# Graph kernel, adjacency build on one core: target one-hots compared in pairs of columns for the first two quarters

## What is computed

```
edge_index = jnp.stack([src, dst])
h = jnp.maximum(_layernorm(x, axis=-1), 0.0)
x = x + _L0_gnn_ref(h, edge_index, ...)        # aggr = segment_sum(x[src], dst)
...
x = x + _L3_gnn_ref(h, edge_index, ...)
```

## Time and profile before

| | us |
|---|---|
| median of 3 runs | 1218.46 (1216.65 to 1220.22) |
| the profiled execution's own time | 1211.5 |
| its span | 1209.6 |
| build, quarter 0 (halves 0 to 13) | 22.8 to 88.5 |
| build, quarter 1 (halves 14 to 27) | 88.5 to 150.0 |
| build, quarters 2 and 3 | 150.0 to 281.5 |

### The profile page before, as it was taken

How to read it: one execution, slowest core, us unless ns; L and a number is a source line. 1 busy time by engine, 2 the same in 40 slices (tenths; PEclk the granted TensorE clock), 3 DMA queues, 4 the chain that set the end, 5 groups by cost and what they waited for, 6 DMA issues and landing times.

```text
span 1209.6 us, 19346 instructions
## 1 busy us (share of the span) xinstructions
PE 1128.0 (93%) x6308; PEld 658.0 (54%) x6308; DVE 678.4 (56%) x2170; ACT 454.7 (38%) x1347; POOL 11.0 (1%) x36
## 2 busy tenths in 40 slices
PE   3778899999999999999899898998899999999997
PEld 3556666665564554545545445545555556544644
DVE  7999999995563235446255355355654325632211
ACT  4559988886562112211301311203521214811100
POOL 1000000000000000000000000000000000000000
PEclk9999899999999999999899999999899999999999
DMA  2100000001101013433134123299942313500001
GB/s 76 24 1 2 2 2 10 1 2 34 22 10 25 19 39 80 91 76 77 39 69 89 33 64 84 61 252 190 211 96 69 85 37 102 132 26 26 16 22 31
DMA packets 208277, 70.33 MB, mean 58 GB/s; under 512 B 180949, under 2 KB 207284, under 8 KB 208174
## 3 DMA queue, kind: packets, MB, share of 16 engines
q1 hardware_dynamic: 124702, 42.31, 16.1%
q10 hardware_dynamic: 83152, 25.52, 9.5%
q0 software_dynamic: 320, 1.22, 0.6%
HBM read 20.71 MB, written 28.26 MB: 40 GB/s over the span
## 4 chain that ended last, share of the span: by engine, by line
PE 81%; DVE 10%; DMA 3%; ACT 2%; issue 2%; ACTq 1%; DVEq 0%; SPq 0%
PE PS L1190 51%; PE PS L894 8%; DVE HPb L758 4%; PE PS L2647 4%; PE PS L883 2%; PE PS L1567 2%; PE PS L859 2%; DMA di_d<-SM 2%; PE PS L2097 2%; PE PS L2103 2%; DVE HPb L709 2%; PE PS L2135 1%; PE PS L1685 1%; PE PS L1235 1%; PE PS L888 1%
## 5 line engine op out<-in xcount | busy, mean ns | idle before, releaser
L1190 PE MATMUL PS<-ADJ,HPb 125*128 125x500 bf16 (+2 forms) x2250 | 447.3, 354 | 0.0
L1190 PEld LDWEIGHTS PS<-ADJ,HPb 125*128 125x128 f16 x2250 | 219.4, 98 | 223.4 <-issue 32.1
L930 ACT CAST ADJ<-PS 126x72 f32 (+7 forms) x784 | 193.4, 316 | 53.8 <-PE PS L894 18.8
L1190 PE MATMUL PS<-ADJ,Zf 125*128 125x500 bf16 (+2 forms) x1050 | 202.1, 352 | 0.0
L894 PE MATMUL PS<-HPb 128*128 128x150 bf16 (+3 forms) x784 | 193.5, 350 | 3.0 <-ACT ADJ L930 2.4
L1190 PEld LDWEIGHTS PS<-ADJ,Zf 125*128 125x128 f16 x1050 | 102.4, 98 | 93.8 <-issue 1.3
L758 DVE TENSOR_SCALAR HPb<-XRf,Zf 128x176 bf16<-128x176 f16 (+2 forms) x588 | 135.8, 289 | 1.7 <-PE PS L894 0.7
L883 PEld LDWEIGHTS PS<-HPb 128*128 128x128 bf16 x642 | 86.3, 142 | 62.5 <-issue 37.5
L1871 DVE CUSTOM_DVE_ANT_0 HPb<-ADJ,HPb 125x625 bf16<-125x625 bf16 x125 | 101.3, 811 | 3.7
L883 PE MATMUL PS<-HPb 128*128 128x25 bf16 x642 | 91.5, 215 | 12.6 <-DVE HPb L758 11.8
L1977 DVE BATCH_NORM_STATS2 WB<-PS 128x6 f32<-128x500 f32 (+2 forms) x28 | 17.7, 630 | 144.8 <-PE PS L2103 144.8
(11 more groups left out here) (340 smaller groups left out, 1077.1 us busy)
## 6 DMA issues: line engine op xcount, KB each, us to landing
adj_d<-ADJ ACTq DMA_DIRECT2D x25, 700.0 KB
HPb<-y_d SPq DMA_DIRECT2D x19, 187.5 KB, 2.5
HPb<-di_d SPq DMA_DIRECT2D x10, 250.0 KB, 3.4
adj_d<-ADJ ACTq DMA_DIRECT2D x25, 81.2 KB
ADJ<-in_x SPq DMA_DIRECT2D x1, 1562.5 KB
q_d<-HPb SPq DMA_DIRECT2D x25, 62.5 KB
HPb<-di_d SPq DMA_DIRECT2D x5, 305.2 KB
HPb<-s_d ACTq DMA_DIRECT2D x5, 250.0 KB, 3.7
```

What stands on the lines that cost most here:

```text
L930: e.copy(to, WPS[group % BANKS][0:PD, t0 * RESTS[q]:t1 * RESTS[q]] .rearrange("p (t d) -> p t d", t=t1 - t0)).then_inc(s_mv, 1)
L1190: mm = e.matmul(accs[q], H[0:PN, t, q, 0:P], cols, start=(t == 0 and (two or q == 0)), stop=(t == NT - 1 and (two or q == 1)), skip_group_ ...
```

## The change

In quarters 0 and 1 (`PAIRED = 2`) one TENSOR_TENSOR compares two columns at once: it reads `IOK[q]`, now with every number stored twice, and the two columns' keys from a new f16 table `KTH[q]`, broadcast along the numbers, and writes the two one-hots interleaved element by element into one slot of the ring. The ring of 7 slots so holds 14 columns. PE reads a column's one-hot as every second element of the slot. Quarters 2 and 3 are as before.

```diff
+    PAIRED = 2
+    IOS = [w * (2 if k < PAIRED else 1) for k, w in enumerate(KWS)]
...
+        def key_pair(q, m):
+            return OHK[m // 2 % RING][:, 0:IOS[q]].rearrange("p (w c) -> p w c", c=2)
+
+        def key_hot(q, m):
+            return key_pair(q, m)[:, :, m % 2] if q < PAIRED else OHK[m % RING][:, 0:KWS[q]]
...
-                    line(e.tensor_copy(IOK[k], iota_i[:, c0:c0 + KWS[k]]))
+                    numbers = iota_i[:, c0:c0 + KWS[k]]
+                    if k < PAIRED:
+                        numbers = numbers.rearrange("p (w o) -> p w o", o=1).broadcast_to([P, KWS[k], 2])
+                    line(e.tensor_copy(IOK[k], numbers))
...
-            tables = ((KT, til_f, (2, 0)), (PT, src_f, (3, 1)), (KGT, key_f, (6, 7)))
+            tables = ((KT, til_f, (6, 7)), (PT, src_f, (3, 1)), (KGT, key_f, (2, 0)))
...
+                keys_told(0)
+                table_out(1)
...
+                table_out(2)
                 e.wait_ge(s_frow, 1)
                 e.copy(IOC, IOP.rearrange("p (n o) -> p n o", o=1).broadcast_to([P, P, HC])).then_inc(s_rowc, 1)
+                table_out(0)
+                keys_told(1)
...
+                    if n == 2 * QS:
+                        e.wait_ge(s_rowc, KR + 13)
                     for m in range(HC):
-                        k = (h * HC + m) % RING
-                        if m % 2 == 0:
-                            e.wait_ge(s_ohx, n0 + m + 2)
+                        free = n0 + m + 2 - (RING if q < PAIRED else 0)
+                        if m % 2 == 0 and free > 0:
+                            e.wait_ge(s_ohx, free)
...
+                        elif m % 2 == 0:
+                            e.tensor_tensor(key_pair(q, n0 + m), IOK[q],
+                                            KTH[q][:, n0 + m - q * KTW:n0 + m + 2 - q * KTW].rearrange("p (o c) -> p o c", o=1)
+                                            .broadcast_to([P, KWS[q], 2]), ALU.is_equal).then_inc(s_oh, 2)
...
-                                              OHK[m % RING][:, 0:NT], start=False, stop=True, skip_group_check=True)
+                                              key_hot(q, m)[:, 0:NT], start=False, stop=True, skip_group_check=True)
...
-                                     OHK[m % RING][:, NTP:KWS[q]], start=(c == 0), stop=(c == GC - 1),
+                                     key_hot(q, m)[:, NTP:KWS[q]], start=(c == 0), stop=(c == GC - 1),
```

More of the change, by code:

```diff
@@ L148, in build @@
         OHW = -(-KWP // 64) * 64
+        assert GC == 2 and RING == HG and all(w <= OHW for w in IOS)
         IOW = sum(KWS[:3]) + P
+        KTW = GC * QG
         SRW = max(RW, HC * P // 2)
@@ L153, in build @@
         HPb = sb("HPb", [P, max(NT * 2 * FW + 2048, RING * OHW + 2 * HC * P + NT * GW, 8 * RW, 60 * P)], BF16)[:, :]
-        XRf = sb("XRf", [P, max(NT * P, RW + SRW + sum(KWS[:2]) // 2 + 8 + P // 2 + GW * NT // 2 + FTW)], F32)[:, :]
+        XRf = sb("XRf", [P, max(NT * P, RW + SRW + sum(IOS[:2]) // 2 + GW * NT // 2 + 2 + FTW)], F32)[:, :]
         Zf = sb("Zf", [P, max(NT * P, 3 * NCH + (NCH + HC) // 2, 25 * P)], F32)[:, :]
@@ L227, in build @@
         c0 = RW + SRW
[L228 to L232, removed]
+        IOK = [XRf[:, c0:c0 + IOS[0] // 2].bitcast(F16),
+               XRf[:, c0 + IOS[0] // 2:c0 + (IOS[0] + IOS[1]) // 2].bitcast(F16)]
+        IOK = [v.rearrange("p (w c) -> p w c", c=2) for v in IOK]
+        c0 += -(-(IOS[0] + IOS[1]) // 8) * 4
+        IOP = HPb[:, 8 * RW + 8 + KTW:8 * RW + 8 + KTW + P].bitcast(F16)
         IOL = XRf[:, c0:c0 + GW * NT // 2].bitcast(F16)
@@ L237, in build @@
         FT = XRf[:, c0:c0 + FTW].bitcast(I32)
+        KTH = [HPb[:, 8 * RW + 8:8 * RW + 8 + KTW].bitcast(F16),
+               WB[:, 4 * P + 6 * NT + 2:4 * P + 6 * NT + 2 + KTW // 2].bitcast(F16)]
         dst_f, src_f, til_f, key_f = (HPf[0:QG, k * RW:(k + 1) * RW] for k in range(4))
@@ L601, in program, with keys_told, table_out @@
             if act:
-                for n, (tab, _, banks) in enumerate(tables):
+                def keys_told(q):
+                    for h in range(GC):
+                        e.wait_ge(s_rowt, h + 1)
+                        e.copy(KTH[q].rearrange("p (g h) -> p g h", h=GC)[:, :, h],
+                               PS[:, tables[0][2][h], q * QG:(q + 1) * QG]).then_inc(s_rowc, 1)
+                def table_out(n):
+                    tab, _, banks = tables[n]
                     for h in range(GC):
@@ L606, in program @@
                          .then_inc(s_rowc, 1)
[L607 to L610, removed]
+                keys_told(0)
+                table_out(1)
+                for h in range(GC):
+                    e.copy(PTH[:, 0:NCH].rearrange("p (g h) -> p g h", h=GC)[:, :, h], PS[:, tables[1][2][h], 0:G])\
+                     .then_inc(s_rowc, 1)
+                table_out(2)
                 e.wait_ge(s_frow, 1)
                 e.copy(IOC, IOP.rearrange("p (n o) -> p n o", o=1).broadcast_to([P, P, HC])).then_inc(s_rowc, 1)
+                table_out(0)
+                keys_told(1)
             e.wait_ge(s_flag, 1)
@@ L887, in half @@
                             else:
-                                e.matmul(CPS[h][:, g * NT:(g + 1) * NT], lhs, OHK[m % RING][:, 0:NT], start=(c == 0),
+                                e.matmul(CPS[h][:, g * NT:(g + 1) * NT], lhs, key_hot(q, m)[:, 0:NT], start=(c == 0),
                                          stop=(c == GC - 1), skip_group_check=True)
@@ L969, in general_build @@
             if role == "pool":
-                e.wait_ge(s_rowc, KR + 9)
+                e.wait_ge(s_rowc, KR + 13)
                 line = Line(e, s_gpool)
```

5 lines of the change are left out of this document (3 added, 2 removed).

## The result

| | before | after |
|---|---|---|
| median of the timed runs, same chip, us | 1218.38 (1216.65 to 1220.22) | 1212.07 (1210.74 to 1212.79) |
| ratio to before, 95% interval | 1 | 0.9949 (0.9935 to 0.9964) |
| profiled execution: own time, span | 1211.5, 1209.6 | 1212.8, 1211.2 |
| quarter 0, us | 65.7 | 58.8 |
| quarter 1, us | 61.5 | 60.8 |

The kernel is faster by 6.3 us. The forecast was 14.7 us (1204), with a range down to a gain of 6.5. The sign is right and the size is less than half. The last four lines use one cut everywhere: a quarter runs from the start of the source one-hots of its first half (line 709 before, 736 after) to the next quarter's, and the build ends where DVE's first 125x1500 instruction starts. (The 131.5 of the earlier trace rows for the last two quarters stops at 281.5; by this cut it is 132.1.)

A forecast was written before the change was run, and what follows sets the result against it. DVE alone was taken to set quarter 0, and DVE with 3.2 us of waits quarter 1. Gains of 9.5 + 5.5 less 0.3 made 14.7, so 1218.5 became 1203.8, said as 1204; range 1199 to 1212.

The forecast's parts named there:

- (a): DVE's paired compare: a pair costs 0.253 us in quarter 0, 0.357 in quarter 1; gains 9.5 and 4.6 of DVE work.
- at 3.5: Length in us forecast for an ordinary half of quarter 0 after the change.
- (b): DVE's pair re-reading one 4-byte word: no penalty taken; the skill page's rule would add 0.12 and 0.19 us per pair.
- (c): PE reading every second element: 0 taken, up to 0.32 ns per moving column allowed; PE hidden behind DVE in both quarters.
- (d): ACT in quarter 1: needs 3.66 us per half against DVE's new 3.88, so hidden by 0.2.
- (e): Ring of 14 columns: 2.3 of quarter 1's 3.2 us of waits stay; quarter 1 takes 56.0 against 61.5, gaining 5.5.
- In halves 1 to 10 it gives nothing: The longer ring brings 0 there, as line 723's add keeps DVE within a pair of the half before.
- (f): Two DMAs of half 11: DVE waits about 0.3 us for the counts, a loss of 0.3 (0 to 0.8).
- (g): Preparation before the build: the larger `IOK` and ACT's moved tables and copies cost 0.
- The gain goes to the end in full: Everything behind the build starts from its last cast, so the whole 14.7 us was to reach the end.
- ACT and PE holding quarter 1: Rival, chance 0.16: ACT and PE pace quarter 1, which gains 1 us or nothing; median 1209.
- slower rival: Two rivals: PE's strided reads at half rate, say 1235 us (0.06); DVE's pair at one element per cycle, 1250 (0.05).

The follow-up runs named there:

- experiment 3: The kernel before, with ACT's second activation per tile left out from tile 4 on: 1214.93 us, ratio 0.9978.
- experiment 8: The changed kernel, with DVE waiting as if the ring still held 7 columns: 1215.83 us in one run, the kernel before beside it 1215.3.
- experiments 10 and 11: Both kernels run once more unedited, for their profiles: before 1217.07 us (one run), after 1211.76 us, ratio 0.9948.

## Why the prediction was right in sign and wrong in size

**(a) The paired compare: right in price, wrong in the sum.** Its pitch of 0.25 and 0.357 is the forecast's. The first half, which has no adds, took 2.75 where 0.98 + 7 x 0.253 is 2.75. The failed step is the half of quarter 0, "at 3.5": it put 0.10 for an add behind each pair, as in the earlier trace rows, where a chain of adds of 0.40 is the longer one. Halves 3 to 7 take 3.8 to 4.2, and quarter 0 gains 6.9 and not 9.2. Some 1.9 of the missing gain lies in halves 2 to 7, for the most part in the chain of adds; another 0.7 is in half 1, whose first add also has to wait for PE to finish half 0. Line 748 and the add's 0.27 in the earlier trace rows were there to be read: 0.355 leaves less than 0.1 between an add's end and the next one's start.

**(b) No penalty for a word that is read again: right.** 441 - 333 = 108 ns for 200 elements is 0.54 ns each, beside the 0.52 forecast. The Trainium skill, Vector Engine (DVE) Microarchitecture Reference, Measured stream behaviour on trn2, keeps a port's full rate to streams that read two or more adjacent words and gives hopping every element 1.73 ns a column. A stream that stays on one word of two keys doesn't pay that: the pitches came out at the 0.25 and 0.357 of the forecast, without the 0.12 and 0.19 that the rule would add.

**(c) PE's reads: right but for a trace,** 5 to 10 ns per matmul by the starts, where 0 was taken. The Trainium skill, Advanced Engine Details and Errata, SBUF Cachelines, asks for at least two hits on a line of 16 bytes to hide the access; a stride of 4 bytes has four, and the trace agrees to within those few ns. The strided weights of the earlier trace rows, 28 bytes apart, do pay (139 against 98 ns).

**(d) ACT: wrong, and the step on which quarter 1 fell.** "A pair of casts 0.30" was read from two that stand between activations. The lines behind it in the same timeline of before said otherwise:

```profile
108.04 1.37 ACT L930 CAST ADJ<-PS 126x120 f32 x6
109.30 0.51 ACT L690 ACTIVATE Zf<-ADJ,SM 125x128 f16<-125x128 f32 x1
```

Six casts in 1.26 are 0.21 each. A half of ACT is 4.33 after, not 3.66, which is over DVE's new 3.88. The cover of 0.2 per half was not there. By its busy time ACT is at 4.16 of 4.35 in such a half, and 0.18 of the rest is the register load.

**(e) The ring and quarter 1: wrong by 4.8.** 56.0 was forecast and 60.8 came. The forecast saw that ACT was behind the 3.2 us of waits, and then let a longer ring take 0.9 of them away and DVE's gain go through in full. The ring was the lesser part: without half of ACT's activations 1.5 to 1.8 of the waits are gone with the ring still at 7 (experiment 3), and the ring of 14 is worth 0.3 to 0.4 in quarter 1 with ACT's full load (experiment 8). DVE got faster and was handed its gain back as waits for line 717. "In halves 1 to 10 it gives nothing" holds but for half 1, which only gives back part of half 0's gain; the forecast gave the ring nothing in halves 0 and 11 to 13 either, and in quarter 0 as a whole it is worth 1.0. At the start of quarter 2 DVE now waits 1.31 us for PE (at 143.09), which the ring of 14 has let fall behind, and half 27 takes 5.72 in place of 4.41. That this loses time is not shown: with the wait of the old ring half 27 takes 4.34, and quarter 1 is no shorter for it (61.20).

**(f) and (g): no cost.** DVE doesn't wait before the counts (line 820 follows its pair without a gap), since the two DMAs' issues were 1.99 apart and began earlier. The build begins at 22.8 to 24.4 us in kernels of either form, so the preparation shows no difference.

**"The gain goes to the end in full": wrong by some 3 us** in the profiles (experiments 10 and 11), and one profiled execution was a poor base: of 8.1 us that the build lost, 7.6 lie in quarters 0 and 1, the other 0.5 in quarter 2, which takes 62.0 or 62.6 in profiles of one kernel. With 3 less behind the build the first two leave 4.6, beside the 6.3 (4.4 to 7.9 by the interval) of the timed runs.

**The rivals.** ACT and PE holding quarter 1 (0.16) was right: it gained 0.7, the rival said 1 or nothing. It gave 1209 and not 1212 because it had quarter 0 gain 9.2. Of the two it was ACT more than PE: its clock makes little difference to an ordinary half (4.31 at 0.61, 4.35 at 1.00), but PE and ACT do wait for each other through the banks, and how much of the 4.33 is that exchange stays open. No slower rival showed anything.

## What to carry to other kernels

- Before an engine is made faster, time the whole cycle of every other engine of the pipeline from one marker to the same marker in the next round, as 107.23 to 111.56 here. A sum of pitches picked from the best spot of the cycle is a lower bound.
- Look for chains of an instruction on its own predecessor (a wait for the last write of the same engine). They cost nothing until the period falls under the duration plus the time to see it done, here 0.27 + 0.13.
- Where a second engine stands close behind, move its side work to a stage with room first, or the new speed is handed over as waits. Here the two edits together gave 9.5 us, the pairs alone 6.3 and the spreading alone nothing, each against the kernel before on its own chip.

## What the runs showed of the hardware

A TENSOR_TENSOR whose second operand re-reads one 4-byte word of two f16 keys goes at 0.54 ns per element. A moving operand that takes every second bf16 element costs PE 5 to 10 ns per matmul of 150 or 250 columns, seen in the starts and not in the modelled durations. A DVE instruction with a computed address, waiting for an earlier one of DVE, started 0.13 us after that one's end, 0.05 of it the register instruction on which the wait stands. Two 128x1 MEMSETs more lengthen such a period by 0.01 us or less (half 4: 3.84, not 3.80, over 7 periods). A register load in ACT's queue (TENSOR_LOAD) took 0.55 us, and the casts behind it weren't issued meanwhile. And 2 us more of a DMA wait on PE (3.49 for 1.51) came with a granted clock of 1.2 GHz behind it, and twelve matmuls took 1.4 us longer; a wait of 2.66 in another kernel had no such dip.
